# Scores of an even and an odd head in the two halves of TensorE's rows, and one mask product for each bank of the first pass

## The reference

```
x = x + attn_a(layernorm(x))      # 16 heads of 8 dims, rotary, causal softmax, biases
x = x + ffn(layernorm(x))         # 8 heads of 64 dims, full softmax, gated mixture of 5 experts
x = x + attn_b(layernorm(x))      # as attn_a, with other weights and rotary angles
x = x + ffn(layernorm(x))
```

## Time and profile before

| | |
|---|---|
| median of 3 runs | 2207.96 us (2207.55 to 2214.34) |
| the profiled execution's own time | 2209.6 us |
| its span, first to last instruction | 2207.9 us |
| busy: PE, DVE, ACT, POOL | 1899.7, 1637.4, 1275.3, 1045.1 us |
| mean granted TensorE clock | 0.945 of full speed |

### The profile page before, as it was taken

How to read it: one execution, slowest core, us unless ns; L and a number is a source line. 1 busy time by engine, 2 the same in 40 slices (tenths; PEclk the granted TensorE clock), 3 DMA queues, 4 the chain that set the end, 5 groups by cost and what they waited for, 6 DMA issues and landing times.

```text
span 2207.9 us, 40511 instructions
## 1 busy us (share of the span) xinstructions
PE 1899.7 (86%) x11328; PEld 913.1 (41%) x11328; DVE 1637.4 (74%) x2950; ACT 1275.3 (58%) x2803; POOL 1045.1 (47%) x1124
## 2 busy tenths in 40 slices
PE   1758998899898889989888998989899898998775
PEld 0323444435354443535444353544434354443433
DVE  4548787877878787787878777787877777796561
ACT  0326657575665757566575756657575665757452
POOL 1214455462635546263554626355462635555433
PEclk8779999999999999999999999999999999999977
DMA  3121212020121202012120201212020121200000
GB/s 95 42 34 30 34 40 35 28 34 17 34 34 40 34 28 35 16 35 33 40 34 28 36 16 36 31 40 34 28 37 21 34 28 39 34 6 13 10 10 5
DMA packets 87623, 68.19 MB, mean 31 GB/s; under 512 B 10720, under 2 KB 83104, under 8 KB 87328
## 3 DMA queue, kind: packets, MB, share of 16 engines
q1 hardware_dynamic: 87456, 66.62, 16.5%
HBM read 32.51 MB, written 10.49 MB: 19 GB/s over the span
## 4 chain that ended last, share of the span: by engine, by line
PE 49%; DVE 29%; issue 12%; ACT 5%; DMA 2%; POOL 1%; DVEq 1%; SPq 0%; ACTq 0%; POOLq 0%; PEldq 0%; PEld 0%
DVE nmaxA L878 6%; PE Y L488 6%; PE S1c L429 4%; DVE ztmp L999 4%; DVE nmaxF L883 4%; PE S1b L429 4%; PE S2a L453 4%; PE M L619 3%; PE S2b L453 3%; PE Y L479 3%; PE S1a L429 3%; DVE rotated L924 2%; PE M L539 2%; ACT Pq L713 2%; PE M L592 2%
## 5 line engine op out<-in xcount | busy, mean ns | idle before, releaser
L1117 POOL TENSOR_TENSOR Z<-Z,ztmp 128x1280 f32<-128x1280 f32 x112 | 324.8, 2900 | 374.7 <-DVE ztmp L999 373.5
L1084 POOL TENSOR_SCALAR_AFFINE_SELECT PT<-PT 128x256 f32<-128x256 f32 (+1 forms) x640 | 248.3, 400 | 395.8 <-ACT PT L698 393.1
L1108 POOL TENSOR_TENSOR Vf<-Vf,ztmp 128x512 f32<-128x512 f32 x256 | 352.5, 1377 | 139.9 <-DVE ztmp L973 134.8
L698 ACT ACTIVATE PT<-S2a 128x512 f32<-128x512 f32 x320 | 191.1, 597 | 152.7 <-PE S2a L447 124.4
L488 PE MATMUL Y<-PT,Vf 128*64 128x512 f32 x1024 | 274.8, 617 | 0.0
L429 PE MATMUL S1a<-Kf,Qf 64*128 64x512 f32 x352 | 216.6, 698 | 6.6 <-ACT Pq L713 4.6
L973 DVE TENSOR_TENSOR ztmp<-xv,wv_s 128x512 f32<-128x512 f32 x256 | 219.7, 858 | 2.8 <-POOL Z L1117 2.8
L429 PE MATMUL S1c<-Kf,Qf 64*128 64x512 f32 x352 | 209.2, 676 | 12.6 <-ACT Pq L713 11.2
L702 ACT ACTIVATE PT<-S2a 128x512 f32<-128x512 f32 x256 | 153.1, 598 | 89.8 <-PE S2a L453 89.6
L698 ACT ACTIVATE PT<-S2b 128x512 f32<-128x512 f32 x320 | 191.3, 598 | 14.1 <-PE S2b L447 13.2
L429 PE MATMUL S1b<-Kf,Qf 64*128 64x512 f32 x320 | 190.8, 678 | 6.5 <-ACT Pq L713 6.5
(11 more groups left out here) (109 smaller groups left out, 3931.5 us busy)
## 6 DMA issues: line engine op xcount, KB each, us to landing
Qs<-parts SPq DMA_DIRECT2D x96, 128.0 KB
Ks<-parts SPq DMA_DIRECT2D x96, 128.0 KB
tab_s<-in_tab SPq DMA_DIRECT2D x16, 512.0 KB, 4.3
xr<-out_x SPq DMA_DIRECT2D x32, 256.0 KB, 2.8
out_x<-res SPq DMA_DIRECT2D x32, 256.0 KB, 2.2
wa_s<-in_wa SPq DMA_DIRECT2D x16, 320.0 KB, 2.9
xl<-out_x SPq DMA_DIRECT2D x16, 256.0 KB, 2.8
out_x<-in_x SPq DMA_DIRECT2D x8, 256.0 KB, 4.7
```

The costliest lines, as they stand in the source:

```text
L698: nc.scalar.activation(PT[:, slot % 2, b, :], t[:, :], ACT.Exp, scale=SCALE_A).then_inc(exps_done.sem, 1)
L1084: last = nc.gpsimd.affine_select(out=v, in_=v, compare_op=ALU.is_ge, fill=0.0, base=0, pattern=pattern, channel_multiplier=-1)
L1108: nc.gpsimd.tensor_tensor(Vf[:, i, :, :], Vf[:, i, :, :], vtmp[:, n % VBUF, :, :], ALU.add).then_inc(v_acc.sem, 1)
L1117: nc.gpsimd.tensor_tensor(Z[:, :, :, :], Z[:, :, :, :], ztmp[:, hh % 2, :, :, :], ALU.add).then_inc(z_acc.sem, 1)
```

## The change

- `Qs` and `Ks` become [128 partitions, 8 head pairs, 512]: rows 0 to 47 hold an even head, 64 to 111 the odd head of the same pair; the maxima's two rows are 48, 49 and 112, 113. The products contract over 48 (pass 1) or 50 (pass 2) rows at partition 0 or 64, so each takes a 64-row half of the array.
- The banks are ordered so that banks b and b+1 (b even) hold the same shapes for an even and an odd head. `pass1` and `pass2` of attention do nothing at odd b and both banks at even b: all score products of the two banks one after the other, the even head's bank first.
- The mask is one product for each bank, over one or two blocks of 128 columns (`maskb2`): 10 for each group in place of 16, with the same number of columns.
- Waits: a pair of pass 1 waits once for the reader of bank n-2 (n the first of the two); a pair of pass 2 waits once for the exponential of bank n-1.
- The 12 scatter DMAs become 24, each of 64 source partitions; the two DMAs of maxima rows per group each write two partitions of one half. The first clearing of `Qs` and `Ks` covers 8 head pairs in place of 16 heads, and the ones are set by two instructions on 32 partitions.

```diff
-    ROWS_P1 = 96
+    ROWS_P1 = NSP * DA
     ROWS_P2 = ROWS_P1 + 2
+    HALF = 64
...
-            BANKS_A1 += [[(h, 3, 0)], [(h, 2, 0), (h, 0, 384)]]
-            BANKS_A2 += [[(h, 0, 0)], [(h, 1, 0), (h, 3, 384)]]
-        BANKS_A1.append([(h0, 1, 0), (h1, 1, 256)])
-        BANKS_A2.append([(h0, 2, 0), (h1, 2, 256)])
+    for h0 in range(0, GA, 2):
+        BANKS_A1 += [[(h, 3, 0)] for h in (h0, h0 + 1)] + [[(h, 2, 0), (h, 0, 384)] for h in (h0, h0 + 1)]
+        BANKS_A2 += [[(h, 0, 0)] for h in (h0, h0 + 1)] + [[(h, 1, 0), (h, 3, 384)] for h in (h0, h0 + 1)]
+    BANKS_A1 += [[(h, 1, 0), (h + 2, 1, 256)] for h in (0, 1)]
+    BANKS_A2 += [[(h, 2, 0), (h + 2, 2, 256)] for h in (0, 1)]
...
-        Qs = sb("Qs", [ROWS_P2, HA, T], BF)
-        Ks = sb("Ks", [ROWS_P2, HA, T], BF)
+        Qs = sb("Qs", [P, HA // 2, T], BF)
+        Ks = sb("Ks", [P, HA // 2, T], BF)
...
                         for r in range(NSP):
-                            sp.dma_start(dst[DA * r:DA * r + DA, :, :],
-                                         parts[:, qk, order[r], :]).then_inc(scattered.sem, 16)
+                            for lo in (0, HALF):
+                                sp.dma_start(dst[lo + DA * r:lo + DA * r + DA, :, :],
+                                             parts[lo:lo + HALF, qk, order[r], :]).then_inc(scattered.sem, 16)
...
-                    if group >= SA and b % GF:
+                    if b % 2:
                         return
...
-                    pe.wait_ge(*s1_free(j, (n if group < SA else n + 1) - len(S1)))
+                    pe.wait_ge(*s1_free(j, n + 1 - len(S1)))
                     if group < SA:
-                        for h, qt, col in BANKS_A1[b]:
-                            hh, keys = GA * group + h, (qt + 1) * P
-                            nc.tensor.matmul(t[:, col:col + keys], Qs[0:ROWS_P1, hh, qt * P:keys],
-                                             Ks[0:ROWS_P1, hh, 0:keys], start=True, stop=False)
-                            last = nc.tensor.matmul(t[:, col + qt * P:col + keys], identb[:, :], maskb[:, :],
-                                                    start=False, stop=True)
-                        last.then_inc(s1_filled.sem, 1)
+                        for i in range(2):
+                            for first, (h, qt, col) in enumerate(BANKS_A1[b + i]):
+                                hh, keys, r = GA * group + h, (qt + 1) * P, HALF * (h % 2)
+                                nc.tensor.matmul(S1[(n - 1 + i) % len(S1)][:, col:col + keys],
+                                                 Qs[r:r + ROWS_P1, hh // 2, qt * P:keys],
+                                                 Ks[r:r + ROWS_P1, hh // 2, 0:keys], start=first == 0, stop=False)
+
+                        for i in range(2):
+                            t, segs = S1[(n - 1 + i) % len(S1)], BANKS_A1[b + i]
+                            blocks = t[:, :].rearrange("p (k c) -> p k c", c=P)
+                            blocks = (blocks[:, 3:4, :] if len(segs) == 1 else blocks[:, 1::2, :]
+                                      if segs[0][1] == segs[1][1] else blocks[:, 2:4, :])
+                            nc.tensor.matmul(blocks, identb[:, :], maskb2[:, 0:len(segs), :],
+                                             start=False, stop=True).then_inc(s1_filled.sem, 1)
...
+                    if slot < SA and b % 2:
+                        return
...
-                    pe.wait_ge(exps_done.sem, exps_done.at(j, n - len(S2)))
+                    pe.wait_ge(exps_done.sem, exps_done.at(j, (n + 1 if slot < SA else n) - len(S2)))
                     if slot < SA:
-                        for h, kt, col in BANKS_A2[b]:
-                            hh = GA * slot + h
-                            last = nc.tensor.matmul(t[:, col:col + T - kt * P], Ks[0:ROWS_P2, hh, kt * P:kt * P + P],
-                                                    Qs[0:ROWS_P2, hh, kt * P:T], start=True, stop=True)
+
+                        for i in range(2):
+                            for h, kt, col in BANKS_A2[b + i]:
+                                hh, r = GA * slot + h, HALF * (h % 2)
+                                last = nc.tensor.matmul(S2[(n - 1 + i) % len(S2)][:, col:col + T - kt * P],
+                                                        Ks[r:r + ROWS_P2, hh // 2, kt * P:kt * P + P],
+                                                        Qs[r:r + ROWS_P2, hh // 2, kt * P:T], start=True, stop=True)
+                            last.then_inc(s2_filled.sem, 1)
...
-            nc.vector.memset(Ks[ROWS_P1:ROWS_P2, :, :], 1.0).then_inc(dve_init.sem, 1)
+            for lo in (0, HALF):
+                nc.vector.memset(Ks[lo + 32:lo + HALF, :, :], 1.0).then_inc(dve_init.sem, 1)
...
-    plain = [h * D + d for d in range(D) for h in range(H)]
-    swapped = [h * D + (d + D // 2) % D for d in range(D) for h in range(H)]
+    plain = [h * D + d for odd in range(2) for d in range(D) for h in range(odd, H, 2)]
+    swapped = [h * D + (d + D // 2) % D for odd in range(2) for d in range(D) for h in range(odd, H, 2)]
```

More of the change, by code:

```diff
@@ L54, in attention_and_mixture @@
     BANKS_A2 = []
-    for pair in range(GA // 2):
-        h0, h1 = 2 * pair, 2 * pair + 1
-        for h in (h0, h1):
-            BANKS_A1 += [[(h, 3, 0)], [(h, 2, 0), (h, 0, 384)]]
-            BANKS_A2 += [[(h, 0, 0)], [(h, 1, 0), (h, 3, 384)]]
-        BANKS_A1.append([(h0, 1, 0), (h1, 1, 256)])
-        BANKS_A2.append([(h0, 2, 0), (h1, 2, 256)])
+    for h0 in range(0, GA, 2):
[3 more added lines that the diff above has]
+    BANKS_A2 += [[(h, 2, 0), (h + 2, 2, 256)] for h in (0, 1)]
     NA_B = len(BANKS_A1)
@@ L97, in attention_and_mixture @@
         identb = sb("identb", [P, P], BF)
-        maskb = sb("maskb", [P, P], BF)
+        maskb2 = sb("maskb2", [P, 2, P], BF)
         wa_s = sb("wa_s", [P, 5, C])
@@ L205, in attention_and_mixture @@
         x_copied = Signal("x_copied", B, 16)
-        consts_cast = Signal("consts_cast", 2)
-        dve_init = Signal("dve_init", 6)
+        consts_cast = Signal("consts_cast", 3)
+        dve_init = Signal("dve_init", 7)
         xlA_loaded = Signal("xlA_loaded", 1, 16)
@@ L316, in rows @@
                     apart(sp)
-                    for i in range(2):
-                        sp.dma_start(Qs[ROWS_P1 + i:ROWS_P1 + i + 1, GA * group:GA * group + GA, :],
-                                     mrowA[i * GA * NT:(i + 1) * GA * NT, :]).then_inc(rowsA_in.sem, 16)
+                    for odd in range(2):
+                        r = HALF * odd + ROWS_P1
+                        sp.dma_start(Qs[r:r + 2, GA // 2 * group:GA // 2 * (group + 1), :],
+                                     mrowA[odd * GA * NT:(odd + 1) * GA * NT, :]).then_inc(rowsA_in.sem, 16)
                 if f_end:
@@ L454, in pass2 @@
                                                        ident[:, :])
-                    last.then_inc(s2_filled.sem, 1)
+                        last.then_inc(s2_filled.sem, 1)
                 def has_values(slot):
@@ L683, in _ @@
             nc.scalar.activation(identb[:, :], ident[:, :], ACT.Copy).then_inc(consts_cast.sem, 1)
-            nc.scalar.activation(maskb[:, :], maskf, ACT.Copy).then_inc(consts_cast.sem, 1)
+            for i in range(2):
+                nc.scalar.activation(maskb2[:, i, :], maskf, ACT.Copy).then_inc(consts_cast.sem, 1)
             def iteration(j, a, f, f_end, a_prep, f_prep):
@@ L872, in maxima @@
                         if len(segs) == 2 and segs[1][1] == qt0:
-                            last = nc.vector.tensor_reduce(nmaxA[:, GA * group + h0:GA * group + h0 + 2, qt0],
+                            last = nc.vector.tensor_reduce(nmaxA[:, h0 % 2, GA // 2 * group:GA // 2 * (group + 1), qt0],
                                                            t[:, :].rearrange("p (h k) -> p h k", h=2), AX.X, ALU.max,
@@ L877, in maxima @@
                             for h, qt, col in segs:
-                                last = nc.vector.tensor_reduce(nmaxA[:, GA * group + h, qt:qt + 1],
+                                last = nc.vector.tensor_reduce(nmaxA[:, h % 2, GA // 2 * group + h // 2, qt:qt + 1],
                                                                t[:, col:col + (qt + 1) * P], AX.X, ALU.max, negate=True)
@@ L894, in split_maxima @@
                     dve.wait_ge(*filled(j, f"rows{before}", 1 if group == 1 else 0))
-                    src = nmaxA[:, GA * group:GA * group + GA, :]
-                    nc.vector.tensor_copy(nmb[:, 0, :, :], src).then_inc(maxA_chain.sem, 1)
+                    src = nmaxA[:, :, GA // 2 * group:GA // 2 * (group + 1), :]
+                    nc.vector.tensor_copy(nmb[:, :, 0, :, :], src).then_inc(maxA_chain.sem, 1)
                     dve.wait_ge(maxA_chain.sem, maxA_chain.at(j, group + 1, lag))
-                    nc.vector.tensor_tensor(nmb[:, 1, :, :], src, nmb[:, 0, :, :], ALU.subtract).then_inc(nmb_ready.sem, 1)
```

(4 more changed lines are left out.)

10 lines of the change are left out of this document (5 added, 5 removed).

## The result

The changed kernel takes 2280.6 us (median of four runs, 2275.0 to 2281.3), the kernel before beside it 2207.8 (2204.8 to 2214.3). The ratio is 1.032 [1.0292, 1.0348]: slower by 72.8 us. Slower was forecast, with 2257 us: +49 us were forecast and +73 came.

A forecast was written before the change was run, and what follows sets the result against it. It took slots 2 and 3 as bound by the ring of PE, DVE and ACT, slot 1 by DVE, 6 and 7 by PE. 2208 + 47 (waits) + 8 (clock) - 6 (start) = 2257 us; own range 2232 to 2282, overall 2195 to 2296.

The forecast's parts named there:

- The ring: Slots 2 and 3, work passed round PE, DVE and ACT: 3.45 to 3.6 us per pair of steps, 2.7 before.
- Delay of the slots: Slot 3 begins 2.25 us later relative to slot 2; slot 3 itself takes 0.8 us more.
- half of a 384 + 128 group overlap: PE's products: only even 128 and odd 384 lie beside each other, 0.37 us for the pair.
- The clock: Half of one more low-clock stretch per iteration from PE's new gaps: 15 x 0.5 = +8 us, bounds 0 and 30.
- Slots 6 to 1: Slots 6, 7, 0 and 1: +0.1 us in all per iteration, bounds -1.5 and +1.5.
- a full drain: PE's row mode changes: 0.16 us each instead of 0.10, 1.4 us more of PE per iteration; not adopted.
- PE's busy time: Sign in the profile after: PE's busy time falls by some 50 us.
- PE is the bound: Rival: PE's shorter stream counts, 15 x -3.3 = -50 and -6, giving 2152 us; chance 0.15.
- The start: Scatter DMAs -3 us and shorter clears -3.5, together -6; first product of pass 1 comes 4 to 6 us earlier.
- two ports of 27 GB/s: Scatter: eight adjacent partitions use two ports, fitting 59 GB/s; halves moving at once would give some 2243 us.
- Iterations counted: Attention and ffn work meet in 15 iterations, so waits cost +47 us and the clock +8 us.
- the clock falls in the new gaps of slot 2 too: Rival: one and a half low-clock stretches more per iteration, 15 x 1.65 = +25, giving 2282 us; chance 0.12.

The follow-up runs named there:

- e3: The kernel before with only pass 2 done in pairs of banks behind one wait for both; 2324.4 us, ratio 1.0543.
- e12: e3 with the ffn pair issued ahead of pass 2 in slots 2 and 3; 2206.0 us, ratio 0.9984.
- e5: The changed kernel with the ffn pair issued ahead of pass 2 in slots 2 and 3, waits unchanged; 2226.2 us, ratio 1.0061.
- e7: The changed kernel with both attention passes one bank a step and the waits of before; 2287.6 us, ratio 1.0335.
- e11: The kernel before with score products cut to 48 and 50 rows, all heads at partition 0, none side by side; 2361.5 us, ratio 1.0706.
- e4: The changed kernel with an extra ffn pair as filler ahead of pass 2's wait at steps 0, 4, 6 of slots 2 and 3; 2324.7 us, ratio 1.0557.
- e1: The changed kernel with pass 2 of attention one bank a step again, waiting for bank n-2; 2223.8 us, ratio 1.0086.
- e2: The changed kernel with pass 1 of attention one bank a step again, pass 2 still in pairs; 2299.2 us, ratio 1.0417.

## Why the prediction was right, and where its sizes were off

- **The ring: right in slot 2, mixed with the clock in slot 3.** Forecast 3.45 to 3.6 us between ffn pairs; measured 3.60 and 3.34 in slot 2, and 3.93, 3.78 and 3.65 in slot 3 (1005.89, 1009.82, 1013.60, 1017.25), where the first is set by PE at half clock and the others follow a wait or PE's own work. The 2.7 us of before, which I took for both slots, hold for slot 2 only; slot 3 had 3.16, 2.85 and 4.06:

```profile
977.86 0.69 PE L429 MATMUL S1b<-Kf,Qf 64*128 64x512 f32 x1
...
981.02 0.69 PE L429 MATMUL S1a<-Kf,Qf 64*128 64x512 f32 x1
...
983.87 0.69 PE L429 MATMUL S1c<-Kf,Qf 64*128 64x512 f32 x1 [0.27 <-ACT Pq L713]
...
987.93 0.69 PE L429 MATMUL S1b<-Kf,Qf 64*128 64x512 f32 x1
```

  e3 shows that the wait alone makes the ring longer, e12 and e5 that the order alone undoes it.
- **Delay of the slots: somewhat too large.** Slot 3 begins 20.35 behind slot 2 (19.14 before), not 21.4: +1.21 for +2.25 forecast. Slot 4 begins 16.80 behind slot 3 (15.66): +1.14 for +0.8. Together 2.35, forecast 3.05. The ring itself was right: from the ffn pair of step 2 to that of step 6 pass 6.94 us (992.87 to 999.81), forecast 7.03. What I had too small is the gain ahead of it: from slot 2's start to the ffn pair of step 2 it was 8.76 us (958.40 to 967.16) and is 7.56 (985.31 to 992.87), 1.20 less where I had 0.3. And I let only half of a 384 + 128 group overlap, 0.37 for the pair, while it takes 0.23 (999.58 to 999.81).
- **The clock: mis-sized, the largest miss in a steady iteration.** I took 0.5 us per iteration. The start of slot 4 alone went from 3.65 to 4.95, +1.30, and the value products that open slot 3 take 0.86 more (1.90 for 1.04). The half-clock time went from 244 to 469 us over the span. Slots 2 to 4 together grew by 4.06 of the 4.43 us, where the terms for ring and clock had 3.55; how much of the 4.06 is ring and how much is clock can't be split cleanly, since in slot 3 the low clock lengthens the ring. The rest is +0.10 in slot 6, +0.34 in slot 7, and 0.56 less 0.63 in slots 0 and 1: 0.37, where I had 0.1.
- **Slots 6 to 1: nearly right.** Slot 6 +0.10, where I took +0.25 for PE's stream. Crossings cost the 0.10 assumed (0.09 and 0.10 in e7 and e11); ten of them per group are paid by the overlap. The rule that I had weighed is the Trainium skill's, *TensorEngine Tiling (Array Packing)*, Key Properties: a change of the tiling mode drains TensorE. With a full drain of 0.16 a crossing, my estimate from the rows, the 32 of e11's slot 6 would be 5.1 us, and 3.17 were measured.
- **PE's busy time: right,** -47.6 for -50; and the rival "PE is the bound" fell: the shorter stream shortened only slot 1 of the steady iteration, by 0.63, just after slot 0 had given 0.56 more.
- **The start: right in kind.** The first product of pass 1 comes 8.6 us earlier (58.17, 66.78 before), forecast 4 to 6. Two clears take 1.76 each instead of 3.47. Of the scatter I had left the rate as it was: it moved 79 to 80 GB/s in the three windows of 4 us from 44 to 56 us, and 59 to 66 in the four from 46 to 62 us before, at the same DMA share of 0.57 to 0.58. The estimate of two ports of 27 GB/s, 54 together, is below all of them, and the 59 that seemed to fit was the lowest window. The wait fell from 22.6 to 18.1. But the stretch up to the first steady iteration gives 13.9 back, which no step had. Of these, 7.9 are in the first pass 1: from its first product to the first transpose of Y it takes 38.1 us (58.17 to 96.29) at a granted clock of 0.59, where it took 30.2 at 0.78. At 180 to 220 us the granted clock is 0.77, and was 1.00.
- **Iterations counted.** 15 x 3.65 - 6 = +49 us was forecast. The 13 steady iterations cost 4.43 each, 57.6, near the 54.8 that I had for 15. Start and end, with the iterations that aren't steady, cost 12.9 more (5.3 and 7.6), where I had a gain of 6: that is most of what the sum is short of.

The rival "the clock falls in the new gaps of slot 2 too" (2282 us) gave nearly the measured time, but that is luck. In slot 2, where it had put the loss, the granted clock is 1.00; the clock fell inside slot 3, at the border to slot 4, in slots 0 and 1 and at the start. With half rows the clock is also low where the old waits stand: 0.913 in e7 and 0.921 in e11, against 0.945; and with the wait for both banks and the swap it is 0.906 in half rows (e5) and 0.947 on all rows (e12). So two things lower it: the new gaps (e3 0.932, e12 0.947) and the half-row products with their crossings (e11). What the clock alone costs in the changed kernel stays open: e4 was to tell and didn't, and no run held the clock and changed nothing else.

Also open is why the parts don't add. Over before, single and single is 77 us (e7), pass 1 paired 19 (e1), pass 2 paired 94 (e2), both 73. Pairing pass 1 brings 58 us beside a single pass 2 and 21 beside a paired one; pairing pass 2 costs 54 or 17. A part of what pairing pass 1 brings lies ahead of the steady iterations: 28.5 us over before there in e7 and 26.8 in e2, but 2.0 in e1 and 5.3 in the changed kernel. As to pairing pass 2, slot 2 pays 1.7 to 1.95 in both cases; most of the difference is in slots 3 and 4. Their half-clock time goes from 4.6 us (e1) to 10.2 (after) in the one case and from 6.3 (e7) to 3.9 (e2) in the other. That fits the clock as the cause, but it is argued, not shown.

## What to carry to other kernels

Before a wait is widened to two buffers, list what the in-order engine has queued behind it. If that is the producer of another engine's ring, issue the producer first: here one swap of two calls was worth some 120 us (e3 to e12), and 18 us even where nothing had been widened. Half-row products have two costs here: each crossing to full rows or back took 0.10 us, and the granted clock was lower with them. They need to overlap and stand together to pay; in every version of this kernel rows padded with zeros to 96 and 98 were the cheaper form. And an engine that is busy 86% isn't the bound of a slot whose end shows it waiting.

## What was not expected of the hardware

- Products issued as even 384, even 128, odd 384, odd 128 started in pairs: both 384 at 999.58, then the 128 at 999.75 and 999.76. The odd 384 started ahead of the even 128 that was issued before it, so by these starts the halves of the array keep an order each, not one for both.
- Crossing between 48 and 128 rows in bf16: 0.10 us each way (e11). The f32 ffn pair in 64 rows shows nearly the same on its way out: its two products start 0.44 apart (996.47, 996.91), and the transposes on all rows follow the second after 0.52 (997.43).

```profile
996.91 0.59 PE L438 MATMUL S1a<-Kf,Qf 64*128 64x512 f32 x1
...
997.43 0.66 PE L542 MATMUL M<-ident,xn 128*128 128x128 f32 x4
```

- 24 transfers of 64 KB, alternating between partitions below 64 and from 64 on, moved 79 to 80 GB/s at the DMA share (0.57 to 0.58) at which 12 of 128 KB to the lower partitions alone moved 59 to 66. Size, number and place changed together, so which of them does it isn't shown.
- Half-row products, with their crossings, lowered the granted clock though PE was busier: 0.921 in e11, with PE busy 2110.9 us, 90% of the span, against 0.945 and 86% before. In its first pass 1 PE was busy 52.83 of 53.32 us at a granted clock of 0.50.
